# A graph network on one core: the front of the program as one stage, with the count by dst, the scans and the weights beside the first edge pass

## The chip, the core and the metric

One NeuronCore of a Trainium2 chip runs the whole program. Its engines are TensorE (PE), VectorE (DVE), ScalarE (ACT), GpSimd (POOL) and the DMA queues, most of them fed by SyncE (SP). The time is device microseconds of one execution; lower is better.

## The reference

Four graph layers with a layer norm after each, on 3125 nodes of 256 numbers and 50000 edges sorted by `dst`. What matters here is the first of them:

```python
deg_out = max(segment_sum(1, src), 1); deg_in = max(segment_sum(1, dst), 1)
x = features
for l in range(3):
    h = x @ fc_w[l].T + fc_b[l]
    f = einsum('ncd,cde->nce', (h.reshape(n, 4, 64) * deg_out ** -0.5), ch_w[l])
    agg = segment_sum(f[src] * edge_w, dst)
    x = relu(agg * deg_in ** -0.5 + ch_b[l]); outs.append(x)
return concatenate(outs) @ mlp_w.T + mlp_b
```

The second layer takes a segment maximum by `dst`, the third is an attention by `dst`, and the fourth takes three segment maxima by `src`. For these last ones the kernel needs the edges ordered by `src`, which it works out itself from counts and ranks.

## The kernel before

**Edge passes.** Edges lie in 392 tiles of 128, four to a group, so 98 groups (`NG`). There are eight passes over the edges, seven by `edge_pass` and one, the attention, of its own: `e0`, `e1`, `e2` are weighted (first layer), then `e3`, the attention, then `e5`, `e6`, `e7`. Per group, POOL issues four indirect gathers of 128 rows from the table `T` (`gather`, into `G`, six sets of buffers); ACT multiplies by the edge weight (`scale`); PE turns the rows into columns in PSUM (`forth`, tile `e_fm`); DVE runs a segmented scan over them (`scan`); PE turns them back (`hither`, tile `e_em`); ACT copies out (`evac`); SP stores the group and fetches the indices of the group six later (`store`, `prefetch`). Between the passes `node_products` multiplies the node rows by weights and writes the next table.

**Order.** `pipelined` writes out each engine's queue: for step s it calls each function with its lead, `fn(s + lead)`, in the order of the arguments. An engine carries out its queue strictly in order, so a function that stands ahead of another in the list holds it up. `forth` has lead 1 and `hither` lead 0: PE does forth(g+1), hither(g), forth(g+2), and so on. hither(g) waits for scan(g).

**Rank work beside a pass.** `rank_beside(layer)` puts extra work among the steps of `e0`, `e1` and `e2`: one rank step k takes four edge tiles, 98 steps in all, 33, 33 and 32 to a pass, one in every third group. It goes round the engines: `one_hots` (DVE), `flip` (PE, eight transposes), `take` (ACT, three copies), `meet` (PE, twelve matmuls), `places` (DVE, on what `meet` left). On PE `meet` stands ahead of `forth` and `hither` in its group (early), `flip` behind them (late). On DVE `places` stands ahead of the scan of its group.

**The front.** Ahead of `e0` stand seven stages, each closed by a barrier of all engines: `constants`; `edge_columns` (loads src, dst, weights of the edges, turns them into columns `SRCF`, `DSTF`, `WE`; the DMA for src is the first of nine); `histogram(0, DSTF)` and `histogram(1, SRCF)`; `src_nodes`; `node_products("n0")`. A histogram makes one-hots of the high digit (98 wide) and low digit (32 wide) of each key on DVE (`one_hot`, 14 tiles at a time, 28 steps), multiplies them tile by tile on PE, keeps all products in `HIST` (ACT), and sums over 392 tiles in one DVE reduction. Beside the second histogram, POOL marks the first edge of each dst node by an indirect write (`mark`, `flag_dst`), and PE turns weights. `src_nodes` runs 32 scans over `HIST`, which only the rank work reads. `n0` makes the first table, `x @ GW[0]` with the factor `norm_out`, while POOL marks by src (`flag_src`).

## Time and profile before

| | us |
|---|---|
| median of 3 runs | 5416.98 |
| range of the runs | 5415.43 to 5417.36 |
| span of the profiled execution | 5421.3 |
| mean granted TensorE clock in it | 0.777 of full |

The page gives for each engine its busy time as a share of the span: PE 63%, DVE 62%, POOL 61%, ACT 35%. None of them is near full over the whole span, so the shares alone don't tell what sets the time: that is read stage by stage. A row of the timeline gives start and duration in us, the engine, the line of the kernel, the operation, what is written from what, the size and the count, and in brackets how long the engine stood idle ahead of it and what ended that. Matmuls are pipelined, so the step from the start of one row to the start of the next tells more than a row's own duration.

### The profile page before, as it was taken

To read this page: it belongs to the slowest core of one execution; us is meant where nothing else is said; L and a number is where in the kernel's file an instruction comes from. 1 tells how busy PE (TensorE), PEld (TensorE's weight loads), DVE (VectorE), ACT (ScalarE), POOL (GpSimd) and SP (SyncE) were. 2 spreads that over 40 slices of the span, in tenths; PEclk is the share of its full clock that TensorE was granted. 3 is DMA by queue.
4 is the path that set the end of the run, shared out by engine and by line. 5 is a ranking of instruction groups with operands and counts; after the bars stand their busy time and mean duration, and the time that the engine had idled before them with its cause. 6 is when DMAs were issued, how large, how long until landed. Compare 5 with 4: busy or idle time off the path is not lost. (4 is left out here: it accounts for less than half of the span.)

```text
span 5421.3 us, 80197 instructions
## 1 busy us (share of the span) xinstructions
PE 3436.3 (63%) x18554; PEld 2760.3 (51%) x18554; DVE 3334.7 (62%) x6781; ACT 1890.6 (35%) x4275; POOL 3323.9 (61%) x3460
## 2 busy tenths in 40 slices
PE   3577777777787866666646664455556555665552
PEld 3456665666566655444534442355545555455451
DVE  8856655666566657999657775644444444444444
ACT  2256654666366643222223332222212222122221
POOL 1367765777477744777456664277752777357771
PEclk9778778788877778999666776777778777677776
DMA  3078875888488844888369995288853888358881
GB/s 89 16 197 235 235 210 151 239 234 234 128 236 234 235 136 137 234 233 234 110 170 241 248 242 152 65 230 236 237 163 103 236 237 236 96 169 235 236 230 52
DMA packets 965249, 1026.24 MB, mean 189 GB/s; under 512 B 312526, under 2 KB 843784, under 8 KB 965168
## 3 DMA queue, kind: packets, MB, share of 16 engines
q1 hardware_dynamic: 801184, 582.41, 36.8%
q0 software_dynamic: 163984, 442.92, 31.3%
q8 instruction: 30, 0.49, 0.0%
q14 instruction: 51, 0.42, 0.0%
HBM read 573.30 MB, written 449.41 MB: 189 GB/s over the span
## 5 line engine op out<-in xcount | busy, mean ns | idle before, releaser
L1146 POOL DMA_INDIRECT WORK<-table,idxbuf x2744 | 2609.6, 951 | 1319.6 <-issue 763.8
L1191 DVE TENSOR_TENSOR_SCAN WORK<-maskbuf,WORK,e_fm 128x512 f32<-128x512 bf16 x1372 | 1681.1, 1267 | 1293.7 <-PE e_fm L1161 1287.4
L1161 PE MATMUL e_fm<-ident,WORK 128*128 128x128 f32 x5488 | 997.2, 340 | 1044.1 <-DMA WORK<-table,idxbuf 717.5
L1161 PEld LDWEIGHTS e_fm<-ident,WORK 128*128 128x128 f32 x5488 | 790.1, 175 | 1218.8 <-DMA WORK<-table,idxbuf 725.2
L1215 ACT ACTIVATE WORK<-e_em 128x512 f32<-128x512 f32 x1372 | 757.1, 588 | 1607.6 <-PE e_em L1170 1491.3
L1170 PE MATMUL e_em<-ident,WORK 128*128 128x128 f32 x5488 | 995.2, 342 | 109.4 <-DVE WORK L1191 109.3
L1170 PEld LDWEIGHTS e_em<-ident,WORK 128*128 128x128 f32 x5488 | 884.6, 184 | 134.7 <-issue 112.4
L1208 ACT ACTIVATE WORK<-WORK,wbuf 128x256 f32<-128x256 f32 x1176 | 501.0, 496 | 605.2 <-DMA WORK<-table,idxbuf 605.2
L1545 POOL DMA_INDIRECT WORK<-table_attention,idxbuf x392 | 378.2, 965 | 189.5 <-issue 109.2
L1575 PE MATMUL att_o<-WORK 128*128 128x264 f32 x784 | 297.1, 543 | 0.0
L993 PE MATMUL n_t<-ident,WORK 128*128 128x128 f32 x450 | 108.9, 329 | 264.2 <-DVE WORK L966 156.3
L993 PEld LDWEIGHTS n_t<-ident,WORK 128*128 128x128 f32 x450 | 52.2, 156 | 339.0 <-DVE WORK L966 164.3
L1575 PEld LDWEIGHTS att_o<-WORK 128*128 128x128 f32 x784 | 199.5, 267 | 47.9
L521 DVE TENSOR_TENSOR ARENA<-ARENA,iota_b 128x128 bf16<-128x128 bf16 (+5 forms) x308 | 187.2, 665 | 1.4 <-DVEq L758 0.7
L1662 ACT ACTIVATE WORK<-att_o 128x264 f32<-128x264 f32 x392 | 151.1, 389 | 78.2 <-PE att_o L1575 73.4
L1559 PE MATMUL att_a<-ident,ARENA 128*32 128x128 f32 x98 | 33.4, 341 | 220.7 <-ACT ARENA L1649 220.1
L798 PE MATMUL e_ra<-ARENA 98*128 (+1 forms) x784 | 171.2, 302 | 0.0
L1329 PE MATMUL bn_ps<-ARENA,ones 128*128 128x256 f32 x300 | 105.0, 522 | 89.0 <-DVE ARENA L1355 79.0
L1559 PEld LDWEIGHTS att_a<-ident,ARENA 128*32 128x32 f32 x98 | 9.7, 99 | 274.9 <-ACT ARENA L1649 273.5
L798 PEld LDWEIGHTS e_ra<-ARENA 98*128 98x128 f32 x784 | 126.5, 203 | 28.8
L1329 PEld LDWEIGHTS bn_ps<-ARENA,ones 128*128 128x128 f32 x300 | 77.4, 266 | 116.6 <-DVE ARENA L1355 87.2
L844 DVE TENSOR_SCALAR ARENA<-iota_b,ARENA 128x128 bf16<-128x128 bf16 x392 | 133.3, 340 | 0.0
(282 smaller groups left out, 4519.9 us busy)
## 6 DMA issues: line engine op xcount, KB each, us to landing
edge_results<-WORK SPq DMA_DIRECT2D x686, 512.0 KB
edge_results_attention<-WORK SPq DMA_DIRECT2D x98, 544.0 KB
WORK<-table,idxbuf POOLq DMA_INDIRECT x2744
maskbuf<-nst_dst SPq DMA_DIRECT2D x294, 128.0 KB
maskbuf<-low_src SPq DMA_DIRECT2D x294, 128.0 KB, 4.9
ARENA<-dst_row SPq DMA_DIRECT2D x98, 256.0 KB
table<-ARENA SPq DMA_DIRECT2D x35, 640.0 KB, 3.2
maskbuf<-low_dst SPq DMA_DIRECT2D x98, 128.0 KB
```

The costliest lines, as they stand in the source:

```text
L521: return eng.tensor_tensor(dst, key[:, ds(t, n)].unsqueeze(2).broadcast_to([P, n, width]), iota_b[:, 0:width].unsqueeze(1).broadcast_to([P ...
L798: last = eng.matmul(pa[:, n * LO:(n + 1) * LO], rank_tf[0:HI, b, cols], HIST[0:HI, ds((k + first) * RB + n, 1), :].rearrange("p o l -> p ( ...
L993: last = eng.transpose(tp[slot][:, k * P:(k + 1) * P], R[:, slot, k * P:(k + 1) * P], ident[:, :])
L1146: eng.indirect_dma_start(G[:, q * GT + k, 0:D], None, T, bass.IndirectOffsetOnAxis(ap=idxbuf[:, q, k:k + 1], axis=0)).then_inc(got[q].sem, 16)
L1161: last = eng.transpose(fm[:, q % 2, h, k * P:(k + 1) * P], G[:, q * GT + k, h * P:(h + 1) * P], ident[:, :])
L1170: last = eng.transpose(em[:, pair, k, h * P:(h + 1) * P], S[:, q % 2, h, (2 * pair + k) * P:(2 * pair + k + 1) * P], ident[:, :])
L1191: last = eng.tensor_tensor_scan(S[:, q % 2, h, :], maskbuf[:, q, :], fm[:, q % 2, h, :], S[:, 1 - q % 2, h, GT * P - 1:GT * P], op0, op1)
L1208: last = eng.activation(G[:, q * GT + k, 0:D], G[:, q * GT + k, 0:D], ACT.Copy, scale=wbuf[:, q, k:k + 1])
L1215: eng.activation(O[:, q % 2, 2 * pair:2 * pair + 2, 0:D], em[:, pair], ACT.Copy).then_inc(pairs, 1)
L1329: last = eng.matmul(dst, ones[0:n, :], src[0:n, t, :], start=t == 0, stop=t == NT - 1)
L1545: eng.indirect_dma_start(G[:, q * GT + k, :], None, T2, bass.IndirectOffsetOnAxis(ap=idxbuf[:, q, k:k + 1], axis=0)).then_inc(got[q].sem, 16)
L1575: eng.matmul(po[:, k, 0:TW], same[:, q % 2, k, :], G[:, q * GT + k, :], start=True, stop=True).then_inc(made, 1)
```

## The change

The seven front stages become one, `setup`, without barriers inside, in which queues are ordered by hand:

- src is loaded first and counted alone. `one_hot_pairs` writes the one-hots of two edges interleaved, so that key, iota and result all have an innermost step of one over two bf16 values (before, the key was float32 and repeated along the innermost dimension). PE reads them with a step of two.
- POOL adds the 28 products up as they come (`added`), 98x448 float32 at a time, in place of DVE's reduction over all 392 tiles; DVE then reduces over 14.
- Between the two halves of the count (14 steps each) PE turns dst and weights and makes `GW` and `GB`.
- Counts reach the nodes' layout by one matmul with a picking matrix, not through DRAM. The products with `x` follow in the same stage; `x` is turned straight, without the copy to `R`.
- The masks by dst come from comparing each edge's dst with its neighbour's (`mask_rows`), so `flag_dst` and its 25 indirect writes go. The 25 for `flag_src` move from `n0` to `n4`, ahead of `e3`.
- The count by dst, the node numbers, the remaining weights and the 32 scans go beside `e0` (`numbers_and_weights_beside`): one-hots of 8 tiles and 8 matmuls in each of the first 49 groups, loads of weights on SP in groups 1 to 3 and 16, a weight turned in every second group, one scan in each of groups 58 to 89. `e0` is written out flat, without a hardware loop.
- The rank work, now without a place in `e0`, goes into `e1` and `e2`, 49 steps each, one in every second group. `meet` moves behind `hither` on PE, `flip` gets lead 1 in place of 2, `take` lead 0 in place of 1, and there are three sets of buffers in place of two.

On PE in a weighted pass with rank work, this stands around the meeting of one rank step (`e_rb`, `e_ra`: rank work; `e_fm`: forth; `e_em`: hither). Before, in the loop of `e0`:

```order
L798 MATMUL e_ra<-ARENA 128x32
L796 MATMUL e_rb<-ARENA 128x128
L797 MATMUL e_rb<-ARENA 128x128
L798 ISA
L798 MATMUL e_ra<-ARENA 128x32
L1155 ISA
L1161 MATMUL e_fm<-ident,WORK 128x128 [waits e0_scanned,e0_scaled]
L1161 MATMUL e_fm<-ident,WORK 128x128 x7
L1165 REGISTER_ALU
L1167 ISA [waits e0_scanned]
L1170 MATMUL e_em<-ident,WORK 128x128 [waits e0_pairs]
L1170 MATMUL e_em<-ident,WORK 128x128 x3
```

And now, in the loop of `e1`:

```order
L1220 MATMUL e_fm<-ident,WORK 128x128 [waits e1_scanned,e1_scaled]
L1220 MATMUL e_fm<-ident,WORK 128x128 x7
L1224 REGISTER_ALU
L1226 ISA [waits e1_scanned]
L1229 MATMUL e_em<-ident,WORK 128x128 [waits e1_pairs]
L1229 MATMUL e_em<-ident,WORK 128x128 x3
L1226 REGISTER_ALU
L1229 MATMUL e_em<-ident,WORK 128x128 [waits e1_pairs]
L1229 MATMUL e_em<-ident,WORK 128x128 x3
L849 ISA
L853 MATMUL e_rb<-ARENA 128x128 [waits e1_taken]
L854 MATMUL e_rb<-ARENA 128x128
```

The meeting stood ahead of forth and hither of its group; it now stands behind both, behind hither's wait on `scanned`.

On DVE in `e1` the order around it is, now (L1250 is the scan, L826 to L833 are `places`, L255 the one-hots):

```order
L1250 SCALAR_TENSOR_TENSOR WORK<-maskbuf,WORK,e_fm 128x512
L826 SCALAR_TENSOR_TENSOR ARENA<-e_rb,upto 128x128 [waits e1_met]
L826 SCALAR_TENSOR_TENSOR ARENA<-e_rb,upto 128x128 x3
L828 TENSOR_TENSOR ARENA<-e_ra,ARENA 128x128
L830 ISA
L831 TENSOR_REDUCE ARENA<-ARENA 128x4 [waits e1_passed]
L832 REGISTER_ALU
L833 ISA [waits e1_passed]
L833 TENSOR_TENSOR BYSRC<-ARENA 128x4
L1247 ISA [waits e1_turned]
```

Before, `places` also stood ahead of its group's scan, but with the one-hots of the next step between the scan of the group in front and it, and with three scans to a rank step; now there are two scans to a step, and the one-hots stand behind the second.

On POOL in the front, before, the marks beside the second histogram and in `n0`:

```order
L650 DMA flag_dst<-ones,first_dst 50176x1 [waits hist1_node_ready]
L650 DMA flag_dst<-ones,first_dst 50176x1 x24
L155 UNCONDITIONAL_BRANCH
L143 UNCONDITIONAL_BRANCH [waits barrier_Pool_Activation_PE_DVE_SP_gather]
L149 ISA
```

And now, the adding up of the products in a loop of 28:

```order
L336 MEMSET WORK 98x448
L337 UNCONDITIONAL_BRANCH
L337 ISA
L339 REGISTER_ALU [waits set_held]
L340 ISA [waits set_summed]
L340 TENSOR_TENSOR WORK<-WORK,ARENA 98x448
L337 REGISTER_ALU
L337 COMPARE_AND_BRANCH
```

POOL's indirect writes are gone from here, and POOL reads the products in SBUF beside DVE's one-hots instead.

```diff
-def pipelined(total, unroll, eng, *steps):
-
-
+def pipelined(total, unroll, eng, *steps, flat=False):
...
-    turns = (total - max(most, 3)) // unroll
+    turns = 0 if flat else (total - max(most, 3)) // unroll
...
-        HIST, key_hi, key_lo = carve(ARENA[:, NT * RW:NT * 3 * RW], ((ET, LO), F32), ((ET,), F32), ((ET,), F32))
-
-        oh_hi, oh_lo, = carve(AGW_BASE, ((2, HB, HI), BF16), ((2, HB, LO), BF16))
+        DB = 2 * GT
...
+        def one_hot_pairs(eng, dst, key, t, n, width):
+
+            shape = [P, n // 2, width, 2]
+            return eng.tensor_tensor(dst, key[:, ds(t, n)].rearrange("p (a b) -> p a b", b=2).unsqueeze(2).broadcast_to(shape),
+                                     iota2[:, 0:width, :].unsqueeze(1).broadcast_to(shape), ALU.is_equal)
...
+                    with eng.Fori(0, steps) as i:
+                        eng.wait_ge(held, i + 3)
+                        eng.wait_ge(summed, i + 1)
+                        eng.tensor_tensor(added[0:HI], added[0:HI], HIST[0:HI, ds(i * HB, HB), :], ALU.add).then_inc(summed, 1)
...
+                    edges(rows_i[:, 0], a["src"], src_in)
...
+                            eng.dma_start(prev_i[first:first + hi - lo, c:c + 1], ends[lo:hi, :]).then_inc(prev_in, 16)
...
+                    def hots(first, turns):
+                        with eng.Fori(0, turns) as i:
+                            for b in range(2):
+                                n = i * 2 + (first + b)
+                                eng.wait_ge(made, n + 1)
+                                one_hot_pairs(eng, oh_hi[:, b], key_hi, n * HB, HB, HI).then_inc(hot_sem, 1)
+                                one_hot_pairs(eng, oh_lo[:, b], key_lo, n * HB, HB, LO).then_inc(hot_sem, 1)
...
+                    hots(0, half // 2)
...
+                    hots(half // 2 * 2, (steps - half // 2 * 2) // 2)
...
+                    eng.wait_ge(summed, steps + 1)
+                    c.link(eng.tensor_reduce(count_src[:, :], added[0:HI].rearrange("p t l -> p l t"), AX.X, ALU.add))
+                    c.link(spread_counts(c, count_src, spread[0:HI, :].rearrange("p (q l) -> p q l", q=4)))
...
+                    c.inc(eng.tensor_tensor(mask_rows[:, 0, :, 1:P], rows_f[:, 1, :, 1:P], rows_f[:, 1, :, 0:P - 1], ALU.is_equal))
...
-                    with eng.Fori(0, steps // 2) as i:
-                        for b in range(2):
-                            eng.wait_ge(made, i * 2 + (b + 1))
-                            one_hot(eng, oh_hi[:, b], key_hi, i * (2 * HB) + b * HB, HB, HI).then_inc(hot, 1)
-                            one_hot(eng, oh_lo[:, b], key_lo, i * (2 * HB) + b * HB, HB, LO).then_inc(hot, 1)
-                    eng.wait_ge(moved, steps + 2)
-                    c.link(eng.tensor_reduce(count[:, :], HIST[0:HI].rearrange("p t l -> p l t"), AX.X, ALU.add))
-
...
-        def dst_nodes_beside(st):
+        def numbers_and_weights_beside(st, name):
...
-            def on_gpsimd(eng):
-                eng.wait_ge(ready, 1)
-                mark(eng, first_dst, flag_dst, marked)
-
-            return dict(sync=on_sync, vector_first=vector_first, vector_last=vector_last, gpsimd=on_gpsimd)
...
+                def loads(g, q, turn):
+                    if g == 1:
+                        eng.dma_start(mlp, a["L0_gnn_mlp_w"].rearrange("(m p) i -> p m i", p=P)).then_inc(raw_in, 16)
...
+                        eng.dma_start(th3, a["L3_gnn_thetas"].rearrange("l (m p) i -> p (l m) i", p=P)).then_inc(raw_in, 16)
...
+                    if g < groups:
+                        if g >= 2:
+                            eng.wait_ge(dmade, g - 1)
+                        one_hot_pairs(eng, dhi[:, g % 2], dkey_hi, g * DB, DB, HI).then_inc(dhot, 1)
+                        one_hot_pairs(eng, dlo[:, g % 2], dkey_lo, g * DB, DB, LO).then_inc(dhot, 1)
...
+                    if groups + 9 <= g < groups + 9 + LO:
+                        lo = g - (groups + 9)
                         c.inc(eng.tensor_tensor_scan(HIST[0:HI, :, lo], ones[0:HI, 0:1].broadcast_to([HI, ET]),
-                                                     HIST[0:HI, :, lo], startv[:, lo:lo + 1], ALU.mult, ALU.add))
...
-        RANKS = -(-(ET // RB) // LAYERS)
+                                                     HIST[0:HI, :, lo], start_src[:, lo:lo + 1], ALU.mult, ALU.add))
...
+        RANKS = ET // RB // 2
...
-            first = layer * RANKS
-            steps = min(RANKS, ET // RB - first)
+            first = (layer - 1) * RANKS
+            steps = RANKS
...
                     def step(g, q, turn):
-                        if q % 3 == phase and not (isinstance(g, int) and g // 3 >= steps):
-                            fn(turn * (SETS // 3) + q // 3, q // 3 % 2)
+                        if q % 2 == phase and not (isinstance(g, int) and g // 2 >= steps):
+                            fn(turn * (SETS // 2) + q // 2, q // 2)
...
-                    return [(at(0, meet), 0)], [(at(0, flip), 2)]
+                    return [], [(at(0, meet), 0), (at(0, flip), 1)]
...
-                    return [(at(0, take), 1)], []
+                    return [(at(0, take), 0)], []
...
-            node_products("n0", stage_copy(X), GW[:, 0], out1, None, out2, table=(AGG, T), marks=(first_src, flag_src))
...
-                edge_pass(f"e{l}", SRCI, (ALU.mult, ALU.add), nst_dst, True, rank_beside(l))
+                edge_pass(f"e{l}", SRCI, (ALU.mult, ALU.add), nst_dst, True, rank_beside(l) if l else numbers_and_weights_beside)
...
-            node_products("n4", None, DF1, copy_to(AGG), TH1, out2, table=(AGG, T), norm=(add_bias,))
+            node_products("n4", None, DF1, copy_to(AGG), TH1, out2, table=(AGG, T), norm=(add_bias,), marks=(first_src, flag_src))
...
-        constants()
-        edge_columns()
-        load_weights, turn_weights = weights_beside()
-        histogram(0, DSTF, load_weights)
-        histogram(1, SRCF, both_beside(turn_weights, dst_nodes_beside))
-        src_nodes()
+        setup()
```

## Rows read from the trace of the kernel before

**Rows 1.** The page's costliest group: count, then busy us, mean ns, idle us.
```profile
L1146 POOL DMA_INDIRECT WORK<-table,idxbuf x2744 | 2609.6, 951 | 1319.6 <-issue 763.8
```
**Rows 2.** Windows: stretch, its length, busy us (count) by engine, PEclk, DMA share, GB/s.
```profile
16.00:104.00 88.00, 38.26 (x394) 35.18 (x394) 81.88 (x66) 33.20 (x42) 1.84 (x2) 1.00 0.36 104
300.00:785.00 485.00, 381.41 (x2306) 319.45 (x2307) 307.29 (x608) 301.91 (x674) 367.71 (x386) 0.80 0.84 232
2110.00:2590.00 480.00, 336.62 (x2280) 238.71 (x2279) 477.45 (x1324) 103.49 (x190) 364.23 (x381) 0.99 0.83 232
```
**Rows 3.** Groups by line and form, 0 to 400 us: count, busy us, mean ns.
```profile
L521 DVE TENSOR_TENSOR ARENA<-ARENA,iota_b 128x1372 bf16<-128x1372 bf16 x56 | 88.6, 1583 | 0.7 <-DVE ARENA L512 0.7
L650 POOL DMA_INDIRECT flag_dst<-ones,first_dst x25 | 43.1, 1725 | 105.3 <-DVEq L673 97.9 <-issue 7.3
L553 DVE TENSOR_REDUCE count<-ARENA 98x32 f32<-98x12544 f32 x2 | 42.8, 21376 | 4.4 <-ACT ARENA L588 4.4
L521 DVE TENSOR_TENSOR ARENA<-ARENA,iota_b 128x448 bf16<-128x448 bf16 x56 | 34.8, 621 | 0.0
L650 POOL DMA_INDIRECT flag_src<-ones,first_src x25 | 24.5, 979 | 83.1 <-POOLq L155 75.8 <-issue 7.3
L351 POOL MEMSET WORK<- 128x1536 f32 x1 | 1.6, 1589 | 0.0
```
**Rows 4.** Timeline of the front and of the first pass's two ends.
```profile
20.13 57.02 DVE L521 TENSOR_TENSOR ARENA<-ARENA,iota_b 128x1372 bf16<-128x1372 bf16 x56 [0.35 <-DVE ARENA L512]
...
124.05 1.35 PE L573 MATMUL hist_ps<-ARENA 128*98 128x32 bf16 x14 [0.69 <-DVE ARENA L521]
...
209.12 29.73 DVE L703 TENSOR_TENSOR_SCAN ARENA<-ones,startv,ARENA 98x392 f32<-98x392 f32 x32 [5.21 <-PEq L155]
...
254.46 0.44 PE L993 MATMUL n_t<-ident,WORK 128*128 128x128 f32 x2
...
279.65 0.44 PE L993 MATMUL n_t<-ident,WORK 128*128 128x128 f32 x2
...
282.47 0.48 DVE L1086 SCALAR_TENSOR_TENSOR ARENA<-GB,norm_out,WORK 128x256 f32<-128x256 f32 x1 [0.38 <-ACT WORK L1081]
...
291.62 0.99 POOL L1146 DMA_INDIRECT WORK<-table,idxbuf  x1 [17.00 <-DMA wbuf<-WE]
...
802.28 0.94 POOL L919 DMA_INDIRECT ARENA<-edge_results,end_sum  x1 [17.14 <-issue]
```
**Rows 5.** Timeline of PE in `e0`, at full clock.
```profile
506.80 1.09 PE L1161 MATMUL e_fm<-ident,WORK 128*128 128x128 f32 x8 [1.57 <-ACT WORK L1208]
507.73 1.04 PE L1170 MATMUL e_em<-ident,WORK 128*128 128x128 f32 x8
508.60 0.22 PE L787 MATMUL e_ra<-identb,ARENA 128*98 128x128 bf16 x1
...
509.79 0.23 PE L788 MATMUL e_ra<-identb,ARENA 128*32 128x128 bf16 x1
...
574.85 0.23 PE L796 MATMUL e_rb<-ARENA 98*128 98x128 bf16 x1 [0.42 <-ACT ARENA L810]
...
576.82 0.41 PE L798 MATMUL e_ra<-ARENA 98*128 x2
```
**Rows 6.** Timeline of PE in `e0`, at half clock.
```profile
590.05 1.91 PE L1170 MATMUL e_em<-ident,WORK 128*128 128x128 f32 x8
591.75 0.31 PE L796 MATMUL e_rb<-ARENA 98*128 98x128 bf16 x1
...
595.32 1.95 PE L1161 MATMUL e_fm<-ident,WORK 128*128 128x128 f32 x8
597.06 1.91 PE L1170 MATMUL e_em<-ident,WORK 128*128 128x128 f32 x8
```
**Rows 7.** Timeline of DVE in `e0`: places, then the two scans of a group.
```profile
517.10 0.29 DVE L769 SCALAR_TENSOR_TENSOR ARENA<-e_rb,upto 128x128 bf16<-128x128 f32 x1 [0.97 <-PE e_ra L798]
...
518.93 2.45 DVE L1191 TENSOR_TENSOR_SCAN WORK<-maskbuf,WORK,e_fm 128x512 f32<-128x512 bf16 x2
```

813 lines of the change are left out of this document (438 added, 375 removed).

## The prediction

> **What bounds the kernel now.** I read first the page's costliest group, then the windows by stage, then the timeline of the front, and last the timeline of single engines inside the first pass. The reader is to see two different programs. In an edge pass POOL is never free: 392 gathers of 951 ns with some 0.3 us of issue between them [rows 1] make 1.25 us each, 490 us in all. The first gather of `e0` starts at 291.6, and POOL's next work, the gather of the next stage, at 802.3, 17.1 us behind the pass's last one [rows 4]: 510.7 us from the one to the other. In the same stretch PE is busy 381 of 485 us and DVE 307 [rows 2]. They have time over, though not much. The front, ahead of 291.6, is DVE's: 81.9 busy of 88 us in the first histogram [rows 2], where the one-hots run 57.0 us [rows 4] and one reduction 21.4 [rows 3]. Nothing of the front lies beside a pass. So whatever the front gives up, the program gets back in full, as long as what is put beside the passes fits into the time that PE, DVE and POOL have over there.
>
> **The front, step by step.** Before, the one-hots of the first histogram start at 20.1 [rows 4]. The new stage needs three loads, not nine, and no barrier; I take 9.5, between 8 and 14. Then come 28 steps. DVE needs 57.0 / 28 = 2.04 us a step now [rows 4]. The two sizes give the rate: 1372 elements in 1583 ns and 448 in 621 ns [rows 3] are 1.04 ns an element and 0.15 us fixed. If the pair layout doubles the rate, the two take 0.87 + 0.38 us, less the 0.17 us that they overlap now (1.58 + 0.62 against 2.04): 1.08. No row shows two bf16 inputs at double rate, so the bounds are 1.08 and 2.04; I take 1.08.
>
> The Trainium skill, "VectorE: DVE Perf Modes", What auto-detection actually checks, says that the engine takes its two-element mode if every tensor is 16-bit with an innermost step of one, which the pairs give and the old form did not. No row here shows it; by it the step is at the lower bound.
>
> PE's 14 products take 1.35 us a step [rows 4]. POOL's addition of 98x448 float32 is in no row. The nearest is a memset, 1589 ns for 1536 elements [rows 3], so 0.46 us for 448; three times that, for two reads and a write, is 1.4. I take 1.0. Does it run beside DVE? The indirect writes for dst took 1725 ns each while DVE made one-hots, those for src 979 beside other DVE work [rows 3]: one-hots and POOL get in each other's way. So I set a step at 1.08 + 1.0 = 2.1 us, between 1.35 (PE alone) and 3.04 (old rate, in turns). 28 steps are 59 us (38 to 85).
>
> The same skill, "SBUF — State Buffer", Who interferes with whom, says that a DVE instruction with two SBUF inputs contends with a POOL instruction that reads SBUF, the later one blocking fully. The 1725 ns agree. By it the step is the sum of both, by their independence 1.35. "GPSIMD Engine Reference", Elementwise, gives 4497 ns for an addition of 2048 float32, which scaled to 448 would be 1.0 us, an estimate by that page.
>
> The two halves of the count are parted by PE's transposes and the products for three layers, 10 us as an estimate (18 matmuls of 256 columns, each waiting for ACT to clear the bank). The reduction over 14, the picking matmul, the root (with four mask instructions ahead of the reciprocal) come to 5: a reduction of 14/392 of 21.4 us is 0.8. So `norm_out` is ready at 9.5 + 59 + 10 + 5 = 83. Four tiles of the products are made by then. The others go at PE's pace, (279.65 - 254.46) / 17 = 1.48 us a tile [rows 4]: 21 tiles are 31 us, with 2 to start, 116. From the last table row to the first gather it took 291.6 - 282.5 = 9.1 us [rows 4]: 125. **The front gives 291.6 - 125 = 167 us**, with 188 at the fast end (38 us for the steps) and 140 at the slow end.
>
> **`e0`.** The removed rank work is replaced by 49 pairs of one-hots, each some 0.75 us by the rate above, 49x8 matmuls, 12 weight turns and 32 scans of 29.73 / 32 = 0.93 us [rows 4]. DVE: two scans take 2.45 us a group [rows 7], of 5.0; with 0.75 or 0.93 it has 1.6 over. PE likewise. The longest stop, some 30 short dependent instructions for the dst numbers, is 6 us, covered by the six sets of gather buffers (30 us); without them it would be paid in full. What POOL loses is another thing: one-hots and two-input scans hold it up. At worst each costs 0.75 us (1725 less 979) [rows 3]: 60 us. But the 33 steps of the pass before cost next to nothing, 493.5 us by POOL for 490. I take 5 for these and 5 for 2.4 MB of weights on SP's queue ahead of the index loads of groups 7 to 9: **+10**, between -2 and +35.
>
> **`e1` and `e2`: the wait that is added.** A rank step now comes every second group, 10.0 us of POOL, and `meet` stands behind `hither`. Follow the queues from hither(2k). It waits for scan(2k). meet(k) waits behind it. DVE's places(k) waits for meet(k), and scan(2k+1) is queued behind places(k). hither(2k+1) waits for scan(2k+1); flip(k+1) and forth(2k+3) are queued behind it, and hither(2k+2) behind these. That is a ring, and no buffer loosens it, since each link is either a datum or the order in a queue. Before, meet stood ahead of hither, so that it ran during a scan, and a third group gave the ring time. At full clock, from starts of rows [rows 5, 7]: hither 508.60 - 507.73 = 0.87; meet 574.85 to 577.23 = 2.38; places 518.93 - 517.10 = 1.83; two scans' halves 2.45; hither 0.87; flip 508.60 to 510.02 = 1.42; forth 0.93; hand-overs 0.1: **10.85 us**, over POOL's 10.0. At half clock [rows 6]: hither 1.70 twice, meet 3.57, forth 1.74, flip 2.1 (1.42 stretched as meet is), the same 1.83 + 2.45 + 0.1: **15.2**. In the ring PE stands idle some 3.5 us of each turn, while DVE does places and the scan; the clock in `e0`, with like stops, was 0.80 [rows 2], which with two levels means half clock for 40% of the time. So 10.85 + 0.4 x 4.35 = 12.6 us a turn. A pass is 49 turns and about 16 us to fill and drain (an estimate, from the 17.1 us [rows 4]): 633 us for 510.7, **+122 each, +244 for both**. Bounds: 548 (+37) at full clock, 761 (+250) at half.
>
> **Edits with one answer.** The marks by src move to `n4`, where POOL had nothing to do: 25 x 1.28 = 32 us beside two products for 25 tiles and a norm; should those be done sooner, the difference is paid. Keys in bf16, one buffer more, `e0` without a loop: nothing.
>
> **Sum.** -167 + 10 + 244 = +87 on the profiled 5421.3. That span is 4.3 above the median of the runs, so on the median 5417 + 87 = **5504**.
>
> **Rivals.**
> - *The ring at full clock.* In `e3` the clock was 0.99 with PE busy 337 of 480 us in an even beat [rows 2]; PE's work in the ring is 7.4 of 10.85 us. For it: the share is as high. Against it: a stop of 3.5 us in each turn, where `e3` has none so long. It gives -167 + 10 + 74 = -83: 5334. Faster.
> - *The passes stay POOL's.* If I misread a wait and the six buffers absorb the chain, `e1` and `e2` stay at 510.7: -157, 5260. For it: PE and DVE have time over on average [rows 2]. Against it: the queues above.
> - *The ring mostly at half clock, and a worse `e0`.* At 14 us a turn +191 each, `e0` +25: 5417 - 167 + 25 + 382 = 5657.
> - *The pairs aren't faster* or POOL starves DVE: the front gives only 140; the forecast becomes 5531. This changes no sign by itself.
> - *Nothing changes on balance:* turns of 11.7 us, +79 each, give 5418. The point from which the change costs time is a turn of 11.7 us.
>
> **How the numbers follow.** Forecast with turns from 11.9 to 13.4 and the front's bounds: 0.70, own range 5435 to 5590. Full clock or near: 0.12, faster. POOL's pace: 0.08, faster. Within 0.2% (11 us, what a measurement here can tell from no change): 0.04. Mostly half clock: 0.06, slower. So faster 0.20, same 0.04, slower 0.76. The range leaves out POOL's pace and the worst case, 0.14, and reaches to the full clock: 5325 to 5590.
>
> **What would show it.** First gather of `e0` near 125; the loop of one-hots at 2.1 us a step, POOL's additions near 1.0 us; 493 to 530 us of gathers in `e0`; in `e1` and `e2` gathers that pause, POOL waiting for index loads, DVE waiting for the meeting's matmul ahead of places for 3 us or more in every second group, and turns of 12.6 us. It is wrong if the gathers of `e1` keep 1.25 us, or if the front ends beyond 150.

## The result, and the profile after

| | kernel before | changed kernel |
|---|---|---|
| median of 4 runs | 5417.1 us (5415.4 to 5417.4) | 5615.0 us (5605.2 to 5622.5) |
| ratio | | 1.0365, 95% interval 1.035 to 1.038 |
| span of the profiled execution | 5421.3 us | 5620.8 us |
| mean granted clock of PE | 0.777 | 0.761 |

Slower, as forecast, but by 198 us where 87 were predicted: the time lies above the range (5325 to 5590). In three other sets of runs the kernel before itself took 7100 to 7180 us, and there the same change is a gain; they stand last among the experiments.

The windows of the changed kernel, in the order of [rows 2] (stretch, its length, busy us and count of PE, PEld, DVE, ACT and POOL, then PEclk, DMA share, GB/s), for `e0`, `e1` and `e3`:

```profile
115.00:626.00 511.00, 307.78 (x1990) 287.32 (x1991) 312.51 (x382) 263.21 (x591) 384.22 (x392) 0.75 0.84 230
720.00:1360.00 640.00, 469.44 (x2599) 378.07 (x2600) 327.30 (x784) 321.61 (x701) 367.52 (x385) 0.74 0.62 174
2300.00:2780.00 480.00, 333.43 (x2257) 237.23 (x2256) 476.37 (x1317) 102.39 (x188) 364.24 (x380) 0.98 0.83 231
```

`e3` is what it was. `e0` still moves 230 GB/s, its POOL being busy 384 us instead of the 374 that 392 gathers took before. `e1` gives POOL the same 368 us of work in 640 us instead of 485, at 174 GB/s. The timeline answers to [rows 4]: the start of the one-hots, the last row of the table, then the first gather of `e0`, of the stage behind it, of `e1`, and of the stages behind `e1` and `e2`.

```profile
9.86 2.26 DVE L261 TENSOR_TENSOR WORK<-ARENA 128x1372 bf16<-128x1372 bf16 x4 [0.35 <-DVE ARENA L493]
...
106.78 0.48 DVE L535 SCALAR_TENSOR_TENSOR ARENA<-GB,norm_out,WORK 128x256 f32<-128x256 f32 x1 [0.60 <-ACT WORK L587]
...
115.76 1.12 POOL L1205 DMA_INDIRECT WORK<-table,idxbuf  x1 [41.78 <-DMA wbuf<-WE]
...
642.65 0.94 POOL L975 DMA_INDIRECT ARENA<-edge_results,end_sum  x1 [16.30 <-issue]
...
716.58 0.94 POOL L1205 DMA_INDIRECT WORK<-table,idxbuf  x1 [42.23 <-DMA wbuf<-WE]
...
1402.18 0.94 POOL L975 DMA_INDIRECT ARENA<-edge_results,end_sum  x1 [32.61 <-issue]
...
2163.34 0.94 POOL L975 DMA_INDIRECT ARENA<-edge_results,end_sum  x1 [32.58 <-SPq L143]
```

For `e1` and `e2` the same marks in the trace of the kernel before, the first gather of each pass and of the stage behind it:

```profile
876.12 0.94 POOL L1146 DMA_INDIRECT WORK<-table,idxbuf  x1 [42.63 <-DMA wbuf<-WE]
...
1385.19 0.94 POOL L919 DMA_INDIRECT ARENA<-edge_results,end_sum  x1 [16.49 <-issue]
...
1458.85 0.94 POOL L1146 DMA_INDIRECT WORK<-table,idxbuf  x1 [42.26 <-DMA wbuf<-WE]
...
1968.63 0.94 POOL L919 DMA_INDIRECT ARENA<-edge_results,end_sum  x1 [16.36 <-SPq L155]
```

| where | how read | measured | predicted |
|---|---|---|---|
| front | first gather 115.8, was 291.6 [rows 4] | -175.9 | -167 |
| `e0` | 642.65 - 115.76 = 526.9, was 510.7 [rows 4] | +16.2 | +10 |
| `e1` | 1402.18 - 716.58 = 685.6, was 509.1 | +176.5 | +122 |
| `e2` | starts at 1476.5; to 2163.3 it is 686.8, was 509.8 | +177.0 | +122 |
| all else | the difference of the spans, +199.5, less these | +6 | 0 |

The miss lies in `e1` and `e2`: 109 us more than predicted there. The front gave 9 more than expected, and `e0` and all else came out 6 longer each. The waits of `e1`, 720 to 1360 us (sum, times, longest):

```profile
DVE ARENA L826 <- PE e_ra L855: 290.4, 46, 6.4
...
POOL WORK L1205 <- DMA wbuf<-WE: 168.6, 53, 5.4
PE e_em L1229 <- DVE WORK L1250: 164.2, 46, 3.7
```

These are the three signs that the prediction had named: DVE waits for the meeting ahead of places (6.3 us a turn), PE's hither waits for the scan (3.6 us a turn), and POOL waits for index loads, up to 5.4 us at a time, where in `e1` of the kernel before no such wait was over 0.3 us. So the ring is there. What it costs a turn is read from the stage: (685.6 - 16) / 49 = 13.67 us. One turn of it, first PE's rows (PE's stop, which the bracket of the first row gives, then hither, flip, forth, hither, meeting, forth, the next stop), then DVE's:

```profile
1000.24 1.97 PE L1229 MATMUL e_em<-ident,WORK 128*128 128x128 f32 x8 [3.54 <-DVE WORK L1250]
1002.00 0.31 PE L844 MATMUL e_ra<-identb,ARENA 128*98 128x128 bf16 x1
...
1003.94 1.97 PE L1220 MATMUL e_fm<-ident,WORK 128*128 128x128 f32 x8
1005.70 1.50 PE L1229 MATMUL e_em<-ident,WORK 128*128 128x128 f32 x8
1007.04 0.22 PE L853 MATMUL e_rb<-ARENA 98*128 98x128 bf16 x1
...
1009.25 1.07 PE L1220 MATMUL e_fm<-ident,WORK 128*128 128x128 f32 x8
1013.85 0.68 PE L1229 MATMUL e_em<-ident,WORK 128*128 128x128 f32 x2 [3.53 <-DVE WORK L1250]
```

```profile
1009.45 0.29 DVE L826 SCALAR_TENSOR_TENSOR ARENA<-e_rb,upto 128x128 bf16<-128x128 f32 x1 [6.32 <-PE e_ra L855]
...
1011.26 2.45 DVE L1250 TENSOR_TENSOR_SCAN WORK<-maskbuf,WORK,e_fm 128x512 f32<-128x512 bf16 x2
```

From start to start: hither 1.76, flip 1.94, forth 1.76, hither 1.34, meeting 2.41, places 1.81, scan and hand-over 2.59; together 13.61. The order and the links are those of the prediction. The clock in three neighbouring stretches of 6.8 us of the same rows:

```profile
1000.20:1007.00 6.80, 6.76 (x32) 5.70 (x33) 2.93 (x4) 4.14 (x9) 4.41 (x5) 0.53 0.64 180
1007.00:1013.80 6.80, 3.32 (x26) 2.42 (x24) 4.13 (x14) 2.74 (x7) 2.84 (x3) 0.98 0.62 168
1013.80:1020.60 6.80, 6.75 (x32) 5.69 (x33) 2.93 (x4) 4.14 (x9) 4.95 (x5) 0.52 0.61 169
```

The clock goes up and down once a turn. It is half (1.2 GHz) while PE works through hither, flip, forth and most of the second hither, behind the stop, and full (2.4 GHz) over the end of that hither (1.34 us instead of the first one's 1.76), the meeting and nearly all of the stop, where PE has nothing to gain from it. The Trainium skill, "TensorE: Matmul & The Clock Gate", HAM oscillation, describes a loop whose compute is parted by a wait and starts cold in each turn; these rows agree, with a clock of 0.53 behind the stop.

### The profile page after: what moved, and what is told of

The parts are those of the page before. It is cut to its first block and busy times, and to the rows that moved or that the text cites. A ratio compares the mean times of both kernels' runs of the same rounds, so it can differ in the third digit from the quotient of the medians.

```text
span 5620.8 us, 78234 instructions
## 1 busy us (share of the span) xinstructions
PE 3501.2 (62%) x18564; PEld 2816.2 (50%) x18564; DVE 3249.5 (58%) x6802; ACT 1870.7 (33%) x4237; POOL 3333.1 (59%) x3471
## 3 DMA queue, kind: packets, MB, share of 16 engines
q1 hardware_dynamic: 788584, 581.90, 35.2%
q0 software_dynamic: 163184, 442.91, 30.3%
## 5 line engine op out<-in xcount | busy, mean ns | idle before, releaser
L1250 DVE TENSOR_TENSOR_SCAN WORK<-maskbuf,WORK,e_fm 128x512 f32<-128x512 bf16 x1372 | 1679.2, 1265 | 1032.8 <-PE e_fm L1220 1016.5
L1220 PE MATMUL e_fm<-ident,WORK 128*128 128x128 f32 x5488 | 1019.3, 346 | 984.8 <-DMA WORK<-table,idxbuf 732.2
L1220 PEld LDWEIGHTS e_fm<-ident,WORK 128*128 128x128 f32 x5488 | 816.1, 179 | 1145.7 <-DMA WORK<-table,idxbuf 724.1
L1229 PE MATMUL e_em<-ident,WORK 128*128 128x128 f32 x5488 | 1051.4, 356 | 457.0 <-DVE WORK L1250 451.6
L1229 PEld LDWEIGHTS e_em<-ident,WORK 128*128 128x128 f32 x5488 | 927.2, 192 | 505.3 <-issue 455.8
L826 DVE SCALAR_TENSOR_TENSOR ARENA<-e_rb,upto 128x128 bf16<-128x128 f32 x392 | 90.6, 287 | 622.8 <-PE e_ra L855 622.8
L1049 PE MATMUL n_t<-ident,WORK 128*128 128x128 f32 x400 | 97.2, 329 | 220.2 <-DVE WORK L1022 157.9
L1056 PE MATMUL n_m<-TURNED,WORK 128*128 128x256 f32 x600 | 180.1, 429 | 0.0
L1060 PE MATMUL n_m<-TURNED,WORK 128*128 128x256 f32 x600 | 159.2, 389 | 0.0
```

The source lines that it names most:

```text
L1056: last = eng.matmul(mps[:, slot, 0:D], XT[:, slot, k * P:(k + 1) * P], w1[:, k, :], start=k == 0, stop=k == 1)
L1060: last = eng.matmul(mps[:, slot, D:D + n2], XT[:, slot, k * P:(k + 1) * P], w2[:, k, :], start=k == 0, stop=k == 1)
L1220: last = eng.transpose(fm[:, q % 2, h, k * P:(k + 1) * P], G[:, q * GT + k, h * P:(h + 1) * P], ident[:, :])
L1229: last = eng.transpose(em[:, pair, k, h * P:(h + 1) * P], S[:, q % 2, h, (2 * pair + k) * P:(2 * pair + k + 1) * P], ident[:, :])
L1250: last = eng.tensor_tensor_scan(S[:, q % 2, h, :], maskbuf[:, q, :], fm[:, q % 2, h, :], S[:, 1 - q % 2, h, GT * P - 1:GT * P], op0, op1)
```

## The experiments

My theory: the ring makes a turn what it is, and PE's stop in it keeps the clock down. The rivals are the amount of work (a rank step every second group is too much), the meeting's place alone, and links longer than I had summed. A stage is read from the first gather of `e1` to the first of the stage behind it, as above, and a turn is that less 16, by 49.

**The ring cut on PE.** The meeting stands in front of forth and hither again, as in the kernel before, but in every second group.

```diff
-                    return [], [(at(0, meet), 0), (at(0, flip), 1)]
+                    return [(at(0, meet), 0)], [(at(0, flip), 2)]
-                    return [(at(0, take), 0)], []
+                    return [(at(0, take), 1)], []
```

> The first experiment's kernel again, on another chip (there, passes with nothing beside them already took 640 us in place of 494, so nothing of the ring could be read). Edit: rank steps still in every second group, but the meeting ahead of forth and hither in PE's queue, flip two groups ahead, take one. Theory of the ring: e1 and e2 about 512 us each, total about 5265. Rival, the amount of work: passes above 600, total above 5450. Rival, that PE's clock stays low and stretches the shorter chain too: 1.70 + 3.57 + 1.83 + 2.45 = 9.6 us at half clock, which still is under POOL's 10.0, so about 512 to 520 as well.

Measured: 5261.9 us, ratio to the kernel before 0.9722 (0.9704 to 0.9739); `e1` takes 509.5 us.

**The ring cut on DVE.**

```diff
-                    return [(at(1, places), 0)], [(at(0, one_hots), 3)]
+                    return [], [(at(1, places), 0), (at(0, one_hots), 3)]
```

> The second experiment's kernel again. Edit: one link of the ring cut on DVE: places of step k behind the scan of group 2k+1, PE's order as in the changed kernel. Theory of the ring: e1 and e2 about 512 to 530 us each, total about 5265 to 5300. Rival, that the meeting's place in PE's queue is what costs: 686 us a pass. Rival, the amount of work: above 600.

Measured: 5255.3 us, ratio 0.9715 (0.9698 to 0.9733). The first gather of `e1` and of the next stage, the stretch 800 to 1180, and the wait ahead of places in 720 to 1200:

```profile
714.73 0.94 POOL L1205 DMA_INDIRECT WORK<-table,idxbuf  x1 [42.56 <-DMA wbuf<-WE]
...
1221.98 0.95 POOL L975 DMA_INDIRECT ARENA<-edge_results,end_sum  x1 [16.42 <-issue]
```

```profile
800.00:1180.00 380.00, 339.84 (x2118) 274.02 (x2115) 273.12 (x646) 256.79 (x567) 287.69 (x304) 0.82 0.85 236
```

```profile
DVE ARENA L826 <- PE e_ra L855: 55.3, 44, 2.7
```

507.3 us, which is POOL's pace: 304 gathers in 380 us. The work is all still there, PE 340 of 380 us busy, at a clock of 0.82, where `e0` of the kernel before had 0.80 [rows 2]. So neither the amount of work nor the meeting's place in PE's queue alone costs the time; the closed ring does, and either cut opens it. Both versions beat both kernels.

**PE kept busy in its stop.**

```diff
+                    def warm(k, b):
+                        for _ in range(32):
+                            eng.matmul(st.fm[:, 0, 0, 0:P], identb[:, :], iota_b[:, :], start=True, stop=True)
-                    return [], [(at(0, meet), 0), (at(0, flip), 1)]
+                    return [], [(at(0, meet), 0), (at(0, warm), 0), (at(0, flip), 1)]
```

> The third experiment's kernel again. Edit: the changed kernel with 32 useless products of 128 columns behind each meeting (1.7 us at full clock, 3.4 at half) in PE's stop. Theory that the clock makes the turn 13.7 instead of 10.85 us: with the stop filled the clock is full and the turn 10.9 to 11.5, e1 and e2 550 to 580 us each, total 5340 to 5400. Rival, the links are longer than I summed even at full clock: turn 13.7 or more, total 5615 or more.

Measured: 5398.8 us, below the kernel before, with 1568 useless products in each pass. `e1` 581.0, the turn 11.53 us (the stretch 800 to 1180):

```profile
800.00:1180.00 380.00, 319.89 (x2911) 269.34 (x2912) 233.72 (x562) 225.03 (x497) 252.48 (x265) 0.95 0.75 206
```

More work makes the ring 2.1 us shorter. The clock is the cause of most that lies above 10.85. Whether it rose because the stop was filled or because PE had more to do in a turn, this run doesn't part.

**Less and more work in the ring.** Three edits of places: its last three operations behind the scan; four more operations of 0.287 us; two more. The diffs are of the first and the second.

```diff
+                    def rest(k, b):
                         eng.tensor_tensor(sel[:, :, :], pa[:, 0:RB * LO]...
-                    return [(at(1, places), 0)], [(at(0, one_hots), 3)]
+                    return [(at(1, places), 0)], [(at(1, rest), 0), (at(0, one_hots), 3)]
```

```diff
+                        for x in range(4):
+                            eng.tensor_tensor(spare[:, x, :], upto[:, :], upto[:, :], ALU.mult)
```

> Edit: the changed kernel; of places only the four sums stay in front of the scan, the selection, the reduction and the subtraction (0.8 us by the rows of the changed kernel) go behind it. Nothing is left out. Theory that the ring is a sum of its links: the turn falls from 13.7 to 12.9 us, each of e1 and e2 from 686 to about 647 us, where the chip lets the changed kernel take 5615. Rival, that the turn is locked to the clock's changes (6.83 us full and 6.83 half in step with the ring): the turn stays at 13.7 us, or falls by far more than 0.8. On a chip like that of the earlier experiments, where passes with nothing beside them take 640 us or more, the passes stay near 700 by either.

> The fourth experiment's kernel again. Edit: four more DVE operations (1.0 us in all) in each places. Taking 0.8 us out of this place left e1 at 686.3 us and lowered the granted clock from 0.74 to 0.58. Theory of a sum of links at a given clock: turn 14.7, each pass 735 us, total 5713. Theory that the clock gives way (a shorter stop is answered by more half clock and a longer one by less): the turn stays within 0.3 us of 13.7, the passes near 686, and the granted clock in the passes rises above 0.74. Rival, that it leaps to the next step: a turn of 17 us, passes above 800.

> Edit: the changed kernel with two more DVE operations in each places (0.57 us); four (1.15 us) took the turn from 13.67 to 15.3 us and the granted clock in e1 from 0.74 to 0.61, while 0.8 us less left the turn at 13.65 with the clock at 0.58. The ring at full clock would be 11.4 us. Theory that the turn is this sum plus 4.35 us times the share of half clock, and that the share is the one with which turn and clock come out in step: 13.7 us a turn (e1 686 us) at a clock near 0.74 to 0.80, or 15.3 us (e1 765) at one near 0.55, nothing between. Rival, that turns grow smoothly with the added work: between them, 14.4 us, e1 near 725.

Measured: 5615.8, 5769.0 and 5691.2 us. The same stretch, 800 to 1180, of the three, in this order:

```profile
800.00:1180.00 380.00, 315.80 (x1560) 251.52 (x1560) 196.61 (x474) 194.48 (x418) 211.81 (x223) 0.59 0.61 174
```

```profile
800.00:1180.00 380.00, 283.49 (x1394) 226.40 (x1395) 194.05 (x511) 173.14 (x375) 190.13 (x198) 0.61 0.55 153
```

```profile
800.00:1180.00 380.00, 280.45 (x1456) 224.62 (x1456) 195.82 (x498) 179.70 (x390) 200.06 (x210) 0.67 0.59 163
```

`e1` takes 686.3, 765.4 and 727.4 us, so the turns are 13.68, 15.29 and 14.52 us.

The expectations price the edits by the operations' own durations (0.8, 1.15 and 0.57 us), but such operations start 0.2 us apart. What the edits do to the ring is read from the first row of places to the start of the scan. On the mean over the turns between 760 and 1240 us that link takes 1.86 us in the changed kernel and 0.85, 2.64 and 2.27 in the three: 1.01 us less, 0.78 and 0.41 more. Here it is with four operations more:

```profile
1011.87 0.29 DVE L826 SCALAR_TENSOR_TENSOR ARENA<-e_rb,upto 128x128 bf16<-128x128 f32 x1 [8.08 <-PE e_ra L857]
...
1014.50 2.45 DVE L1252 TENSOR_TENSOR_SCAN WORK<-maskbuf,WORK,e_fm 128x512 f32<-128x512 bf16 x2
```

Taking work out gave nothing: the 1.01 us came back as a clock of 0.59 instead of 0.75. Putting 0.78 us in cost 1.6 us and also lowered the clock, so my expectation there, that a longer stop would be answered by a higher clock, was wrong, and a sum of links at a fixed clock doesn't give 1.6 either. With 0.41 us the mean turn is 14.5, which is what the rival of smooth growth had said (727 us, it said 725), though it had the size of the edit wrong; of the theory that only 13.7 or 15.3 can be, nothing is left as a statement on the mean. Single turns do differ, though. The starts of places, read from the timelines of `e1` between 760 and 1240 us, are apart, over and over:

| kernel | turns in a row, us |
|---|---|
| changed | 13.6 or 13.7, all |
| 1.01 us less | 14.4, 13.3, 13.4 |
| 0.41 us more | 15.8, 14.4, 14.0, 13.8 (now and then three of them) |
| 0.78 us more | 14.5, 16.2 |
| kept busy | 11.0, 12.5, 10.9 (now and then two of them) |

In each of these the turns repeat in a pattern. In the last row two turns of three take 10.9 to 11.0 us, the 10.85 that I had summed for the full clock, and the third meets a stretch at half. Two neighbouring stretches of two turns each, of the ring with 0.41 us more, with 112 instructions of PE in both, show the same thing from the clock's side:

```profile
990.40:1021.10 30.70, 23.05 (x112) 18.43 (x112) 15.41 (x39) 13.86 (x30) 16.16 (x17) 0.61 0.57 159
1021.10:1048.40 27.30, 19.92 (x112) 16.01 (x112) 14.30 (x39) 13.75 (x30) 14.01 (x15) 0.75 0.60 166
```

**Both at once**: the useless products and the shorter places.

> The kernel of the experiment before once more, since every pass there took 640 us or more, with or without a ring. Edit: 32 useless products in PE's stop, and the last 0.8 us of places behind the scan. Nothing is left out. Theory that the 0.8 us were taken back by the clock alone: with the clock held up the turn goes from 11.5 to 10.7 us, e1 from 581 to about 541 us, total about 5318. Rival, that those 0.8 us are not on the ring: 581 us and 5399.

Measured: 5356.1 us, `e1` 552.8, the turn 10.95 us at a clock of 0.96 (800 to 1180). With the clock held up the same edit is worth 0.58 of its 1.01 us; alone it was worth nothing. So it was on the ring, and the clock had taken it back. Why only 0.58, one turn shows: first DVE's rows (places, the first of the moved operations, the second scan, the next places), then the hither behind the second scan:

```profile
1010.66 0.29 DVE L826 SCALAR_TENSOR_TENSOR ARENA<-e_rb,upto 128x128 bf16<-128x128 f32 x1 [3.58 <-PE e_ra L857]
...
1013.87 0.27 DVE L830 TENSOR_TENSOR ARENA<-e_ra,ARENA 128x128 f32<-128x128 f32 x1
...
1015.62 2.44 DVE L1257 TENSOR_TENSOR_SCAN WORK<-maskbuf,WORK,e_fm 128x512 f32<-128x512 bf16 x2
...
1021.52 0.29 DVE L826 SCALAR_TENSOR_TENSOR ARENA<-e_rb,upto 128x128 bf16<-128x128 f32 x1 [3.46 <-PE e_ra L857]
```

```profile
1018.19 1.09 PE L1236 MATMUL e_em<-ident,WORK 128*128 128x128 f32 x8 [0.24 <-DVE WORK L1257]
```

A second ring has taken over. It goes from places over both scans of the turn, with the moved operations and the one-hots between them, then hither and the meeting, 10.86 us from places to places, and the moved work stands on it. In `e1` (720 to 1240) PE's hither waits for a scan 81 times here, about twice a turn, and 43 times with the useless products alone.

All turns together; the sum by the prediction's links is the full-clock sum plus 4.35 us times the share of half clock, 2 x (1 - clock). The full-clock sum is 10.85 with the measured change of the link in it:

| ring | full-clock sum | clock | sum at that clock | turn measured |
|---|---|---|---|---|
| changed kernel | 10.85 | 0.75 | 13.03 | 13.67 |
| 1.01 us less | 9.84 | 0.59 | 13.41 | 13.68 |
| 0.41 us more | 11.26 | 0.67 | 14.13 | 14.52 |
| 0.78 us more | 11.63 | 0.61 | 15.02 | 15.29 |
| kept busy | 10.85 | 0.95 | 11.29 | 11.53 |
| kept busy, 1.01 less | 9.84 | 0.96 | 10.19 | 10.95 |

The turn measured lies 0.2 to 0.8 us above this sum in all six. It spreads the half clock evenly over PE's links, which the changed kernel doesn't (its row is 0.64 short), and the last row belongs to the second ring. The clock that goes with them was not mine to choose: it changes with the ring's length.

**The front.** One run with the old layout of the one-hots, one with POOL's additions behind the loop instead of beside it.

```diff
-                                one_hot_pairs(eng, oh_hi[:, b], key_hi, n * HB, HB, HI).then_inc(hot_sem, 1)
+                                one_hot(eng, oh_hi[:, b], key_hi, n * HB, HB, HI).then_inc(hot_sem, 1)
```

```diff
+                    eng.wait_ge(held, steps + 2)
                     with eng.Fori(0, steps) as i:
-                        eng.wait_ge(held, i + 3)
```

> Edit: the changed kernel with the one-hots of the first histogram in the old layout (14 one-hots side by side, the key broadcast over the innermost axis) in place of pairs of edges. Nothing is left out. If the pairs are what lets DVE make them in 1.1 us instead of 2.0: a step goes from 1.87 us to between 2.04 (DVE alone, POOL's addition beside it) and 3.0 (in turns), the first gather of e0 moves from 115.8 by 28 times that, to between 121 and 148; I expect it in turns, 2.9 us and 145. Rival, that PE or the waits set the step: 1.87 and 116.

> Edit: the changed kernel with POOL's 28 additions of the histogram behind the last of the 28 steps instead of beside them. Nothing is left out. If DVE's one-hots and POOL's additions go in turns (1.1 + about 0.8): without the additions the step falls from 1.87 us to PE's 1.35, the one-hots end 14 us sooner, and 28 additions of 0.98 us (27.4 us) follow: the first gather of e0 at about 129. Rival, that they run beside each other and the step is set by the chain of waits between the engines: the step stays at 1.87 and the first gather comes at about 143.

Measured: first gather at 140.8 and at 135.1, total 5640.1 and 5637.9 us. Groups by form, 5 to 110 us of the changed kernel, then 5 to 140 us of the old layout and of the additions behind:

```profile
L340 POOL TENSOR_TENSOR WORK<-WORK,ARENA 98x448 f32<-98x448 f32 x28 | 32.8, 1170 | 31.9 <-ACT ARENA L559 31.2 <-POOL WORK L340 0.8
L261 DVE TENSOR_TENSOR WORK<-ARENA 128x448 bf16<-128x448 bf16 x28 | 28.6, 1023 | 0.0
L261 DVE TENSOR_TENSOR WORK<-ARENA 128x1372 bf16<-128x1372 bf16 x28 | 25.6, 915 | 8.9 <-PE set_wide L423 8.6 <-DVE ARENA L493 0.4
```

```profile
L255 DVE TENSOR_TENSOR WORK<-ARENA,iota_b 128x1372 bf16<-128x1372 bf16 x28 | 59.8, 2135 | 8.1 <-PE set_wide L423 7.8 <-DVE ARENA L493 0.4
```

```profile
L340 POOL TENSOR_TENSOR WORK<-WORK,ARENA 98x448 f32<-98x448 f32 x28 | 27.5, 981 | 56.3 <-ACT ARENA L559 51.0 <-POOL WORK L340 5.4
L261 DVE TENSOR_TENSOR WORK<-ARENA 128x1372 bf16<-128x1372 bf16 x28 | 24.4, 872 | 14.8 <-PE set_wide L423 14.4 <-DVE ARENA L493 0.4
L261 DVE TENSOR_TENSOR WORK<-ARENA 128x448 bf16<-128x448 bf16 x28 | 10.8, 384 | 0.0
```

Left alone, the pairs take 872 and 384 ns, for 1583 and 621 in [rows 3]. Beside POOL's addition the small one takes 1023 ns instead of 384, and the addition 1170 instead of 981. A step, from one start of PE's products to the next, goes from 1.87 us to 1.37, PE's pace, once the additions are gone. They then cost 1.18 us each in a row, not 0.98, because 0.20 us lie between two that hang on each other; so the move loses 19 us, six more than I expected. In the old layout a step takes 2.82 us. So both are shown: the pairs give 0.95 us a step, and DVE and POOL hold each other up for at least 0.5, since PE sets the step without them.

**The weight loads of `e0`**, one a group over eight groups instead of eight in three (on top of the ring cut on DVE):

> Edit: places behind the scan (as before), and in e0 the eight weight loads that SP issued in groups 1 to 3 go out one a group in groups 1 to 8, with the turns of the weights from group 14 on instead of 8. Nothing is left out. Theory: the stop that the gathers of e0 make in groups 7 to 13 (1.483 us a gather instead of 1.25, 6.4 us in all) comes from index loads queued behind these weights; spread they leave it, e0 falls from 525.5 to about 519 us, the total from 5255 to about 5249. Rival, that the stop is the bandwidth of 2.4 MB of weights wherever they are: no change, 5255.

Measured: 5257.6 us, ratio 0.9719 (0.9706 to 0.9732), no change. POOL's wait for index loads in groups 7 to 13 of `e0`, 1.5 us in the kernel before, is in the changed one and in this one:

```profile
POOL WORK L1205 <- DMA wbuf<-WE: 7.2, 4, 3.5
```

```profile
POOL WORK L1210 <- DMA wbuf<-WE: 6.6, 4, 2.7
```

Spreading the loads over eight groups doesn't take the stop away, so the theory that they stand too close together in SP's queue fails. The rival, the bytes of the weights wherever they stand, fits, but no run leaves them out, so it isn't shown.

**The runs beside which the kernel before took 7178, 7162 and 7101 us.** They are eight. There passes with nothing beside them took over 600 us too, so the ring can't be read from them. The changed kernel itself was among them:

> The changed kernel itself, unaltered, beside the kernel before on the same chip, since the first four experiments ran on a chip on which the kernel before takes 7178 us in place of 5417 and every pass of 392 gathers 640 us or more, also those with nothing beside them. If this chip is like the first (before 5417): 5615, ratio 1.0365. If it is like the second (before 7178, passes held up by the DMAs): the ring of 13.7 us a turn, 671 us a pass, is close to what the passes take there anyway, so the front's gain of 175 us is kept and the ratio is about 0.97.

Measured: 6834.9 us, ratio 0.9543 (0.9502 to 0.9584): there the change is a gain. A window of a late pass with nothing beside it, then two of the waits in it for nothing that the profile shows ("issue"); the last fence is a window of such a pass in the changed kernel's profile of the result.

```profile
4460.00:5080.00 620.00, 280.36 (x1512) 245.60 (x1512) 230.40 (x188) 106.44 (x186) 362.84 (x383) 0.65 0.63 179
```

```profile
PEld e_em L1229 <- issue: 195.4, 58, 13.0
...
ACT WORK L1274 <- issue: 82.8, 31, 30.3
```

```profile
3710.00:4190.00 480.00, 276.53 (x1504) 246.49 (x1505) 230.33 (x188) 107.09 (x186) 363.24 (x384) 0.73 0.83 232
```

A pass with nothing beside it needs 620 us there for what took 480. PE's weight loads and ACT stand still up to 13 and 30 us with no releaser shown. Why is open. The expectation speaks of passes held up by the DMAs; the page of the profile has their packets busy for 29.0% and 23.9% of 6830 us (the two large queues), against 35.2% and 30.3% of 5621, which is no more time. `e1` took 754 us and not 686, but the passes with nothing beside them grew more, and the first gather of `e0` came at 115.2 as before. The edits shown above, in these runs:

> Edit: the changed kernel with a rank step still in every second group, but in the old order in PE's queue: the meeting ahead of forth and hither, flip two groups ahead of its meeting, take one. Nothing of the work is left out. Theory of the ring (each scan of an odd group waits for a meeting that is queued behind a hither that waits for the scan before): the ring is cut, the longest chain is then hither 0.9 to 1.7 us + meeting 2.4 to 3.6 + places 1.8 + scan 2.45, which is 7.6 to 9.6 us a turn and under POOL's 10.0; e1 and e2 go from 686 us back to about 512 each, the total from 5615 to about 5265. Rival, the amount of work (a rank step every second group is simply more than PE and DVE can take beside a pass): the passes stay above 600 us and the total above 5450.

Measured: 6900.0 us, ratio 0.9614 (0.9567 to 0.9661).

> As the first experiment: the meeting in front of forth and hither, flip two groups ahead, take one; rank steps in every second group as before. Theory of the ring: where the chip lets a pass run at POOL's pace (before at 5417), e1 and e2 fall from 686 us to about 512 each and the total is about 5265. Rival, the amount of work: above 600 a pass, above 5450. On a chip with slow DMAs: about what the first gave, ratio 0.96.

Measured: 6907.3 us, ratio 0.9644 (0.9554 to 0.9733).

> Edit: the changed kernel with one link of the ring cut on the other engine: DVE does places of step k behind the scan of group 2k+1 and not ahead of it; PE's order stays. Nothing is left out. Theory of the ring: the scan no longer waits for the meeting, e1 and e2 about 512 to 530 us each, total about 5265 to 5300. Rival, that the meeting's place in PE's queue is what costs (PE held up while it waits for the factors): nothing changes, 686 us a pass. Rival, the amount of work: above 600 us a pass.

Measured: 6889.3 us, ratio 0.9594 (0.9549 to 0.9638).

> Edit: the changed kernel with 32 useless products of 128 columns in bf16 behind each meeting, on PE, into a bank that nobody uses then; 1.7 us at full clock, 3.4 at half, in the stop of 3.5 us that PE has there. Theory that the clock makes the turn longer than 10.85 us (PE is granted half clock over hither, flip, forth and hither, because it stood still ahead of them): with the stop filled the clock is granted in full, a turn is 10.9 to 11.5 us, e1 and e2 550 to 580 us each, total about 5615 - 2 x 120 = 5375. Rival, that the ring's links at full clock are themselves longer than I summed: the turn stays at 13.7 us or grows by what the products add, the total is 5615 or more.

> Edit: the changed kernel with four more DVE operations of 128 elements (some 0.25 us each, 1.0 in all) in each places, between the sums and the selection; they change nothing. Theory that the ring's length is a sum of its links: the turn goes from 13.7 to 14.7 us, each pass from 686 to 735, total 5713. Rival, that the turn is locked to the clock's changes (6.83 us full, 6.83 half by the trace, in step with the ring): the longer stop is taken out of or added to the half-clock stretch in steps, the turn stays at 13.7 (less than 0.3 us more) or leaps by far more than 1.0.

Measured: 7036.5 and 6926.7 us.

> Edit: two earlier edits together: 32 useless products in PE's stop, and the last 0.8 us of places behind the scan. Nothing is left out. Each alone: the products took the turn from 13.67 to 11.5 us at a clock of 0.93; the 0.8 us alone gave nothing, the clock fell from 0.74 to 0.58. Theory that the 0.8 us were taken back by the clock and by nothing else: with the clock held up they count in full, the turn goes from 11.5 to 10.7 us, e1 from 581 to about 541 us, total about 5318. Rival, that those 0.8 us are not on the ring at all: 581 us and 5399 as with the products alone.

> Edit: the changed kernel with 12 useless products of 128 columns behind each meeting in place of 32 (0.64 us at full clock, 1.3 at half). Theory that PE's standing still sets the share of half clock, by degrees: something between the changed kernel (0.74, 13.67 us a turn) and 32 products (0.93, 11.5 us); about 0.8 and 12.9 us, e1 about 648 us. Rival, a threshold: nothing (686 us) or all (581 us).

Measured: 6978.1 and 6808.7 us. The second is the edit of the useless products with `range(12)`.

Where these expectations name a total, it was missed by 1,200 us and more, but for the ratios of about 0.97 and 0.96 that two of them named for such a case (0.954 and 0.964). They decide nothing on the ring, and nothing above rests on them. In these runs the cut ring is no better than the closed one: with the meeting ahead `e1` took 786 us in the same set. How the turn moves with 12 products stays open.

## Why the prediction was wrong, and where right

- **Which way**: right. The front gives 176 us and the added wait takes 353 back; the ring stood in the queues before it stood in a trace.
- **The front**, -167 predicted, -175.9 measured. One-hots from 9.86 (9.5 predicted), a step 1.87 us (2.1), 10.6 us between the halves on PE (10), 7.5 from the end of the one-hots to `norm_out` (5), `norm_out` at 78 instead of 83, a row of tiles every 1.09 us (1.48), 9.0 from the last to the first gather (9.1). So 9 us is what is left of misses of both signs. The one-hots and the addition were priced right (0.87, 0.38 and 0.98 us when each is alone); the step is shorter than their sum of 2.23, and than the 2.1 forecast, because the large one-hot still overlaps a part of the addition. The Trainium skill, "SBUF — State Buffer", Who interferes with whom, says that a DVE instruction with two SBUF inputs contends with a POOL instruction that reads SBUF; the runs agree, with 1023 ns for the small one-hot beside the additions and 384 without. The Trainium skill, "VectorE: DVE Perf Modes", What auto-detection actually checks, gives 16-bit tensors with a step of one the two-element mode; the runs agree, 872 ns against 1583.
- **`e0`**, +10 predicted, +16.2 measured. The 392 gathers grew from 374 to 384 us, 10 us (5 predicted), and POOL waited 5.7 us more for index loads in groups 7 to 13 (5 predicted, for the weights; that they are the cause isn't shown).
- **`e1` and `e2`**, +122 each predicted, +176 and +177 measured. This is the step that failed, and in it one term: "half clock for 40% of the time", spread evenly over the ring's PE work, 0.4 x 4.35 = 1.74 us on 10.85. In the trace the four PE links behind the stop take 6.80 us for 4.09 at full clock, +2.71, and the meeting runs at full; 10.85 + 2.71 = 13.56 of the 13.61 measured. The share was taken from the mean of `e0` of the kernel before, a pass without a ring. But the place of the low clock could be read there too: the half clock of [rows 6] begins near 583.6, 1.1 us behind the end of a stop of 2.98 us. In the ring of the changed kernel it falls on the links behind the stop, which the turn waits for, while the full clock is spent on the stop. The bounds of 10.85 and 15.2 held; my forecast's own upper turn of 13.4, and 0.06 for a turn near 14, did not. The row of that stop:

```profile
582.50 1.09 PE L1161 MATMUL e_fm<-ident,WORK 128*128 128x128 f32 x8 [2.98 <-ACT WORK L1208]
```

- **The range.** The prediction says that its own range, 5435 to 5590, takes in turns from 11.9 to 13.4 and the front's bounds of 188 and 140 us. It takes in the turns alone. With the front's bounds it is about 5416 to 5611, and the time measured lies outside that too.
- **The rival of the full clock** was not what happened, but 32 useless products a turn bring most of it about: 581 us for `e1`, where it had said 548.
- **The rival of POOL's pace** happens as soon as one link is cut: 5255 to 5262 us, where it had said 5260.
- **The marks in `n4`**, nothing predicted: 2291.4 - 2163.3 = 128.1 us for the stage, which took 128.2 before (2096.8 - 1968.6): no wait for them.

## What to carry to other kernels

Before rank steps or any side work get closer together, follow each wait through both queues until it closes on itself: a ring costs its full length in every turn however much time each engine has over on average, and one link moved behind another instruction opens it. When a ring is shortened, look for the next one. Ask where in the turn the low clock falls, and don't take the mean clock of a stage without a ring: here the PE links behind the stop ran at half and the meeting at full. And where taking work out of such a loop gives nothing, look at the granted clock before concluding that the work was not on the path.

## What was not expected of the hardware

- The ring and the clock fall into step: 13.7 us in every turn of the changed kernel, and patterns of two, three or four turns in the others. The mean turn is 13.7 us with 10.85 and with 9.84 us of links at full clock (clock 0.75 and 0.59). Whether other rings settle like this was not tried.
- 32 useless products a turn behind the meeting, 1.8 us where they run at full clock, are worth 105 us in `e1`.
- In the runs beside a kernel before of about 7150 us, PE and ACT stop now and then with no releaser shown, and the verdict on this change turns round (0.954 instead of 1.0365).
